# Expert stage of a graph and expert layer: slots of 128 lanes in split float32r, or two experts of 64 seats side by side in native float32

## The chip, the cores and the metric

The kernel runs on one core of one Trainium2 chip (trn2). The metric is the device time of one execution in microseconds. Of the kernel before there are three runs: 924.34, 924.97 and 926.14 us, median 924.97 us.

## The reference

The layer takes x, 384 tokens of 1024 float32, and 12288 typed edges. After a layer norm it adds an attention over the graph (16 heads, a mask built from the edges) and a linear attention with elu features to x. Then a mixture of experts is added to the layer norm of that sum:

```python
sel_logits = jnp.einsum('nd,ed->ne', xt, expert_sel)
gates = jax.nn.sigmoid(sel_logits)
sel_val, sel_idx = jax.lax.top_k(gates, N_HEADS)
gate_full = jnp.zeros_like(gates).at[jnp.arange(N)[:, None], sel_idx].set(sel_val)
scores = jax.nn.relu(jnp.einsum('nd,edf->nef', xt, keys))
scores = scores * gate_full[:, :, None]
out = jnp.einsum('nef,efv->nv', scores, values)
```

There are 32 experts, each with keys of 1024x512 and values of 512x1024 in float32 (2.1 MB each, 4.2 MB together), and each of the 384 tokens goes to 4 of them: 1536 places. On the inputs used, the reference's own routing gives four experts 65, 65, 69 and 84 tokens, and the other 28 at most 56.

## The kernel before

The work runs in one order on all engines: eleven projections of 1024x1024 weights, the attention, the last projections (o0 and o1), a router, and the expert stage. Weights come through SyncE's DMA queue (SP) in chunks of 1 MB. float32 weights and activations are each split in two float32r parts, a high part that ScalarE (ACT) copies and a low part that VectorE (DVE) gets by subtraction; `mm3` (lines 1210 to 1214) multiplies high by high, high by low and low by high, three matmuls for one.

**Router** (lines 1097 to 1161 on DVE). It counts the tokens of each expert and gives each expert one slot of 128 lanes, and a further one for every 128 tokens more. No expert has over 128 tokens, so there are 32 slots. A table says for each slot which token sits in which lane (`gidx`) and with what gate (`tabf`). `slotx` has the expert of each slot, `slots` the loop's end.

**Expert stage, by slots.** For slot s:
- POOL gathers the slot's rows of the normed tokens from HBM by an indirect DMA (`gather`, L643 to L646) into `xg`.
- PE turns them (`x_T`, L1434: eight 128x128 transposes). ACT and DVE evict them as a high and a low part (`xgTh`, `xgTl`).
- `do_keys` (L1419): eight blocks of `mm3` with 512 columns. ACT takes relu and gate (`hsb`), PE turns that (`h_T`, L1440: four transposes), ACT and DVE split it (`hTh`, `hTl`).
- `do_values` (L1424), once for each half of the 1024 outputs: four blocks of `mm3` each.
- ACT evicts y (`ysb`, L828), and POOL adds it to the rows of `out` in HBM by an indirect DMA that adds (L654), masked by lane.

Each megabyte of weights is split by ACT (L724) and DVE (L953), two quarter instructions a chunk, ahead of the matmuls. `pe_slot` (L1443) writes the order out: keys of slot s+1, `x_T` of slot s+2, values of slot s with `h_T` of slot s+1 in their midst. The loop takes two slots a round.

**Chunks.** There are 8 chunk buffers (`raw` and `raw_x`) and 8 split buffers. SP loads the first four expert chunks as soon as the last projection's chunks are split, the next four when the attention is done (`s_pv`), and the others as buffers are split (L536, L564). Between them `rows_out` writes `acc` (the sum before the experts) to `out` and the normed rows to `xt_dram`.

**Attention.** Here native float32 matmuls stand already. `values_of` (L459 to L465) multiplies for two heads at a time, with 128x64 weights each, one head's result in the partitions 0 to 63 of a PSUM bank and the other's in 64 to 127, 384 columns:

```python
for c in range(NT):
    for side in range(2):
        h = 2 * hp + side
        last = nc.tensor.matmul(ps[7][head_rows(side), 0:N], v2[:, c, h * HD:(h + 1) * HD], pT[:, h % PTS, c, :],
                                start=(c == 0), stop=(c == NT - 1))
```

Of the kernel before, what the change touches and what calls it, by code (L numbers as in the profile page):

```python
# [14 lines left out]
P = 128  # L15
# [35 lines left out]
AHEAD = 4  # L51
STEPS = PAIRS * NT
XRAW = 8
XSUB = 8
XLEAD = 4
LANE_STEP = 16
# [48 lines left out]
def gps_layer_kernel(nc, x, edges, etw, W, cols, rows, selT, keys, values, C, xt_dram, out):  # L105
# [3 lines left out]
    with ctx:  # L109
# [9 lines left out]
        arena = sb("arena", [P, 3 * 6144 + 3 * 3072 + 32 + NT * N + D], F32)  # L119
# [7 lines left out]
        BIV = MASK + NT * N * 4  # L127
        xnh, xnl = at("xnh", [P, DC, N], FR, A0), at("xnl", [P, DC, N], FR, A0 + 12 * KB)
# [25 lines left out]
        raw_x = [at(f"raw_x{r}", [P, 4, HALF], F32, A1 + 8 * KB * r) for r in range(3)] + [at("raw_x3", [P, 4, HALF], F32, F2)]  # L154
        wh_x = [at(f"wh_x{r}", [P, 2, HALF], FR, A0 + 8 * KB * r)[:, :, :] for r in range(3)]
        wl_x = [at(f"wl_x{r}", [P, 2, HALF], FR, A0 + 8 * KB * r + 4 * KB)[:, :, :] for r in range(3)]
        xgTh = [at(f"xgTh{p}", [P, DC, P], FR, A2 + 8 * KB * p) for p in range(2)]
        xgTl = [at(f"xgTl{p}", [P, DC, P], FR, A2 + 8 * KB * p + 4 * KB) for p in range(2)]
        hTh = [at(f"hTh{p}", [P, EF, P], FR, A2 + 16 * KB + 4 * KB * p) for p in range(2)]
        hTl = [at(f"hTl{p}", [P, EF, P], FR, A2 + 18 * KB + 4 * KB * p) for p in range(2)]  # L160
# [14 lines left out]
        inslot_h = at("inslot_h", [P, NT, TOPK, SLOTS], F16, route + 7 * KB)  # L175
        slot1h_h = at("slot1h_h", [P, NT, TOPK, SLOTS], F16, route + 9 * KB)
        picked = at("picked", [P, NT, TOPK, NE], F32, route + 11 * KB)
        lane1h_h = at("lane1h_h", [P, NT * TOPK, P], F16, route + 13 * KB)
        cmp = at("cmp", [P, SLOTS - NE, NE], F32, F1)
        lane1h = at("lane1h", [P, NT * TOPK, P], F32, F1 + 2 * KB)  # L180
        tabf = at("tabf", [P, SLOTS], F32, F2 + 8 * KB)
        m8 = at("m8", [P, NT, 8], F32, F2 + 8 * KB + 256)
        pos = at("pos", [P, 4, NT * TOPK], F32, F2 + 8 * KB + 384)
        gidx = at("gidx", [P, SLOTS], I32, F2 + 9 * KB)
        slotx = at("slotx", [P, SLOTS], I32, F2 + 9 * KB + 256)
        slot1h = at("slot1h", [P, NT, TOPK, SLOTS], F32, F2 + 9 * KB + 512)
        acc = sb("acc", [P, NT, D], F32)
        raw = sb("raw", [P, RAW, 4, HALF], F32)
        wh = sb("wh", [P, SUB, 2, HALF], FR)
        wl = sb("wl", [P, SUB, 2, HALF], FR)  # L190
# [4 lines left out]
        wh_x.append(at("wh_x3", [P, 2, HALF], FR, MASK)[:, :, :])  # L195
        wl_x.append(at("wl_x3", [P, 2, HALF], FR, BIV)[:, :, :])
        ysb = [at("ysb0", [P, D], F32, F1 + 8 * KB)[:, :], etmp[:, :, :].rearrange("p a b -> p (a b)")]
# [27 lines left out]
        pcol = sb("pcol", [P, 1], I32)  # L225
# [5 lines left out]
        x_banks = banks[:, 2:4, :].rearrange("p b (c t) -> p (b c) t", t=P)  # L231
        y_banks = [banks[:, 4 + 2 * p:6 + 2 * p, :].rearrange("p b n -> p (b n)") for p in range(2)]
# [4 lines left out]
        s_load = [sem(f"s_load{r}") for r in range(XRAW)]  # L237
# [51 lines left out]
        s_x0h = sem("s_x0h")  # L289
        s_x0l = sem("s_x0l")  # L290
# [5 lines left out]
        s_xhi = sem("s_xhi")  # L296
        s_xlo = sem("s_xlo")
        s_h = sem("s_h")
        s_hT = sem("s_hT")
        s_hhi = sem("s_hhi")  # L300
        s_hlo = sem("s_hlo")
        s_ye = sem("s_ye")
        s_sc = sem("s_sc")
        s_scd = sem("s_scd")
# [7 lines left out]
        def nth_split(s):  # L312

            return s + 1 + (AHEAD if s >= jobs["o1"]["sub"] else 0)

        def nth_expert_split(k):
            return (jobs["o1"]["sub"] if k < AHEAD else SUBS) + k + 1

# [12 lines left out]
        def attention_act(act, split_out, split_ahead):  # L331
# [24 lines left out]
            for i in range(STEPS + 6):  # L356
                if 0 <= i - 3 < STEPS:
                    turned_even(i - 3)
                if i < STEPS:
                    exps(2 * i)  # L360
                    exps(2 * i + 1)
                if 0 <= i - 1 < STEPS and normed_by_act(2 * i - 1):
                    normed(2 * i - 1)
                if i == SPLIT_STEP:
                    split_out()
                if i - 4 == STEPS - 1:
                    act.wait_ge(s_t, 2 * STEPS)
                    split_ahead()
                if 0 <= i - 4 < STEPS and (i - 4) % NT == NT - 1:
                    pair_hi((i - 4) // NT)  # L370
# [21 lines left out]
        def attention_dve(dve, split_out, split_ahead):  # L392
# [13 lines left out]
            for i in range(STEPS + 6):  # L406
# [10 lines left out]
                if i - 5 == STEPS - 1:  # L417
                    split_ahead()
# [89 lines left out]
        raw_of = [raw[:, r, :, :] for r in range(RAW)] + [t[:, :, :] for t in raw_x]  # L508
        wh_of = wh_x + [wh[:, r, :, :] for r in range(SUB)]
        wl_of = wl_x + [wl[:, r, :, :] for r in range(SUB)]  # L510
# [3 lines left out]

        def x_load_done(c, j):

            r = c % XRAW
            return 16 * ((CHUNKS // RAW if r < RAW else 0) + c // XRAW + 1) + 16 * j


        @block.sync
        def _(sp):
# [12 lines left out]
            def expert_half(src_ap, e, half, c):  # L535
                sp.dma_start(raw_of[c % XRAW], src_ap[bass.ds(e, 1), half].rearrange("a p k n -> p (a k) n"))\  # L536
                    .then_inc(s_load[c % XRAW], 16)

            def expert_chunks(src_ap, e, c, j):

                for half in range(2):
                    sp.wait_ge(s_lo, SUBS + 2 * (c + half - XRAW + 1) + 16 * j)
                    expert_half(src_ap, e, half, c + half)


            def rows_out(sp):
                for t in range(NT):
                    sp.wait_ge(s_free, o1_done + t)
                    sp.dma_start(out[t * P:(t + 1) * P, :], acc[:, t, :]).then_inc(s_out, 16)
# [3 lines left out]
            ahead = [src_ap[e, half] for src_ap, e in ((keys, 0), (keys, 1), (values, 0), (keys, 2), (values, 1), (keys, 3))  # L553
                     for half in range(2)]
            for c, chunk in enumerate(ahead):
                if c < RAW:
                    sp.wait_ge(s_lo, nth_split(2 * (CHUNKS + c - RAW) + 1))
                elif c == RAW:
                    sp.wait_ge(s_pv, PAIRS)
                elif c >= XRAW:  # L560
                    if c == XRAW + 2:
                        rows_out(sp)
                    sp.wait_ge(s_lo, nth_expert_split(2 * (c - XRAW) + 1))
                sp.dma_start(raw_of[c % XRAW], chunk).then_inc(s_load[c % XRAW], 16)  # L564
            sp.wait_ge(s_slots, 1)
            last = sp.value_load(slots[0:1, 0:1], min_val=PAIRS_MIN - 1, max_val=PAIRS_MAX - 1)
            c = len(ahead)
            with sp.Fori(0, last - 1) as j:

                e = [sp.value_load(slotx[0:1, bass.ds(2 * j + q, 1)], min_val=0, max_val=NE - 1) for q in range(2, 6)]  # L570
                expert_chunks(values, e[0], c, j)
                expert_chunks(keys, e[2], c + 2, j)
                expert_chunks(values, e[1], c + 4, j)
                expert_chunks(keys, e[3], c + 6, j)
            e = [sp.value_load(slotx[0:1, bass.ds(2 * last + q, 1)], min_val=0, max_val=NE - 1) for q in range(2)]
            expert_chunks(values, e[0], c, last - 1)
            expert_chunks(values, e[1], c + 2, last - 1)
# [3 lines left out]
        def _(pool):  # L581
# [66 lines left out]
            def pool_slot(j, p, count, ahead):  # L648
                s = 2 * j + p
                nc.gpsimd.tensor_copy(pcol[:, :], gidx[:, bass.ds(s, 1)]).then_inc(s_pch, 1)  # L650
                pool_wait(s_pch, count + 1)
                pool_wait(s_ye, s + 3)
# [3 lines left out]
                if ahead:  # L656
                    pool_wait(s_xT, s + 3)
                    gather(s + 4, p, count + 2)
                pool_wait(s_sc, 16 * s + 16)
                pool.sem_inc(s_scd, 1)  # L660

# [10 lines left out]
            last = pool.value_load(slots[0:1, 0:1], min_val=PAIRS_MIN - 1, max_val=PAIRS_MAX - 1)  # L672
            pool.sem_inc(s_scd, 2)
            pool.wait_ge(s_out, 16 * NT)
            pool.wait_ge(s_xT, 1)
            gather(2, 0, 4)
            pool.wait_ge(s_xT, 2)
            gather(3, 1, 5)
            with pool.Fori(0, last) as j:
                for p in range(2):  # L680
                    pool_slot(j, p, 4 * j + 2 * p + 5, True)
# [840 lines left out]
```

## Time and profile before

| | |
|---|---|
| median of 3 runs | 924.97 us |
| span of the profiled execution, first to last instruction | 920.8 us |
| PE busy | 878.7 us (95%) |
| PE weight loads busy | 736.1 us (80%) |
| DVE busy | 655.5 us (71%) |
| ACT busy | 536.9 us (58%) |
| POOL busy | 333.4 us (36%) |
| DMA, mean over the span | 227 GB/s, 209.36 MB |

The profile gives one execution by its span; it has no total time of its own, so the span is set against the median of the runs. The attention ends at about 442 us, o1 at 467 us, and the expert stage's first matmul starts at 497 us. PE is busy nearly everywhere, so its share says little of a single stage; the stage from 497 us on is read by its windows and by the order of PE's instructions. A matmul's duration in the profile is longer than its distance to the next, since matmuls are pipelined: where they stand back to back the distance from start to start is what counts. A native float32 matmul stands in the trace as two records.

### The profile page before, as it was taken

The numbers are of one execution on the slowest core, as the hardware profiler recorded it, in microseconds if no ns is written. First come the engines' busy times: TensorE is split into PE (matmuls) and PEld (weight loads), VectorE is DVE, ScalarE is ACT, GpSimd is POOL, SyncE is SP. The second block draws the span as 40 slices with busy tenths as digits, with TensorE's granted clock in tenths as the row PEclk, the third lists the DMA queues.
The fourth block names the chain that finished last, engine by engine and source line by source line (L and its number), as shares of the span: only waits on it lengthen the run. The fifth ranks groups of instructions, "written<-read, shape, count | busy, mean of one in ns | idle before, by whom it ended". The sixth has DMA issues, their size and how long they took to land.

```text
span 920.8 us, 13930 instructions
## 1 busy us (share of the span) xinstructions
PE 878.7 (95%) x4462; PEld 736.1 (80%) x4462; DVE 655.5 (71%) x1040; ACT 536.9 (58%) x701; POOL 333.4 (36%) x295
## 2 busy tenths in 40 slices
PE   6999999999999999999989989999999999999992
PEld 6987888889889999655766868887888888888882
DVE  7589857534344543685776969889889889989980
ACT  3454312423323322686333968888888888898870
POOL 2042344444444100686003324443324444333341
PEclk9999999999999999999988989999999999999997
DMA  9935432243333533110482989999999999999931
GB/s 353 375 137 183 138 138 92 92 138 138 98 132 138 188 98 132 47 47 1 151 352 76 359 300 343 360 370 362 358 359 359 367 362 370 361 363 365 359 110 22
DMA packets 41638, 209.36 MB, mean 227 GB/s; under 512 B 13136, under 2 KB 13520, under 8 KB 18816
## 3 DMA queue, kind: packets, MB, share of 16 engines
q1 hardware_dynamic: 26496, 186.66, 53.5%
q0 software_dynamic: 14240, 21.38, 8.4%
q10 hardware_dynamic: 864, 0.83, 0.3%
q8 instruction: 22, 0.36, 0.2%
q14 instruction: 16, 0.13, 0.0%
HBM read 209.63 MB, written 21.20 MB: 251 GB/s over the span
## 4 chain that ended last, share of the span: by engine, by line
PE 75%; DMA 11%; DVE 5%; POOL 3%; issue 3%; ACT 1%; POOLq 0%; ACTq 0%; DVEq 0%
PE ps L1212 22%; PE ps L1214 21%; PE ps L1213 21%; DMA out_dram<-etmp,pcol 3%; DMA xg<-xt_dram,gcol 3%; DMA out_dram<-ysb,pcol 3%; PE ps L1434 3%; PE ps L463 2%; POOL out_dram L654 1%; PE ps L439 1%; PE ps L452 1%; PE ps L1440 1%; POOL pr L429 1%; PE ps L1294 1%; DMA ei<-in_edges 1%
## 5 line engine op out<-in xcount | busy, mean ns | idle before, releaser
L714 ACT ACTIVATE wh<-raw 128x1024 fp32r<-128x1024 f32 x88 | 93.0, 1060 | 208.0 <-PE ps L1214 207.7
L896 DVE TENSOR_TENSOR wl<-raw,wh 128x1024 fp32r<-128x1024 f32 x88 | 108.1, 1229 | 131.5 <-ACT wh L714 131.1
L627 POOL DMA_INDIRECT plane<-code,idx x96 | 99.8, 1040 | 122.4 <-DMA plane<-code,idx 96.5
L1212 PE MATMUL ps<-wh_x,hTh 128*128 128x512 f32 x248 | 103.5, 417 | 0.0
L1212 PE MATMUL ps<-wh,xgTh 128*128 128x512 f32 x248 | 98.2, 396 | 0.0
L1214 PE MATMUL ps<-wh_x,hTl 128*128 128x512 f32 x248 | 98.2, 396 | 0.0
L1213 PE MATMUL ps<-wl,xgTh 128*128 128x512 f32 x248 | 97.9, 395 | 0.0
L1214 PE MATMUL ps<-wh,xgTl 128*128 128x512 f32 x248 | 97.8, 394 | 0.0
L1213 PE MATMUL ps<-wl_x,hTh 128*128 128x512 f32 x248 | 97.8, 394 | 0.0
L1212 PE MATMUL ps<-xnh,wh 128*128 128x384 f32 x256 | 86.8, 339 | 0.9 <-DVE xnl L1002 0.9
L1214 PE MATMUL ps<-xnh,wl 128*128 128x384 f32 x256 | 86.6, 338 | 0.0
L1213 PE MATMUL ps<-xnl,wh 128*128 128x384 f32 x256 | 86.4, 338 | 0.0
L953 DVE TENSOR_TENSOR wl<-raw,wh 128x1024 fp32r<-128x1024 f32 x64 | 76.2, 1223 | 12.3 <-ACT wh L724 12.1
L953 DVE TENSOR_TENSOR wl<-raw_x,wh 128x1024 fp32r<-128x1024 f32 x64 | 76.3, 1223 | 11.5 <-ACT wh L724 11.4
L953 DVE TENSOR_TENSOR wl_x<-raw,wh_x 128x1024 fp32r<-128x1024 f32 x64 | 76.7, 1219 | 5.1 <-ACT wh_x L724 4.8
L953 DVE TENSOR_TENSOR wl_x<-raw_x,wh_x 128x1024 fp32r<-128x1024 f32 x64 | 76.4, 1217 | 2.8 <-ACT wh_x L724 2.7
L650 POOL COPY pcol<-gidx 128x1 int32 x32 | 17.7, 552 | 162.4 <-DMA out_dram<-etmp,pcol 81.9
L429 POOL TENSOR_SCALAR pr<-pr,mx 128x384 f32<-128x384 f32 x40 | 49.3, 1252 | 74.1 <-DVE mx L390 74.1
L724 ACT ACTIVATE wh_x<-raw 128x1024 fp32r<-128x1024 f32 x64 | 67.6, 1061 | 14.2 <-PE ps L1214 13.8
L724 ACT ACTIVATE wh_x<-raw_x 128x1024 fp32r<-128x1024 f32 x64 | 67.4, 1060 | 12.1 <-PE ps L1214 10.7
L724 ACT ACTIVATE wh<-raw 128x1024 fp32r<-128x1024 f32 x64 | 65.6, 1055 | 10.7 <-PE ps L1214 10.2
L724 ACT ACTIVATE wh<-raw_x 128x1024 fp32r<-128x1024 f32 x64 | 65.7, 1054 | 9.6 <-PE ps L1214 9.0
(230 smaller groups left out, 2023.9 us busy)
## 6 DMA issues: line engine op xcount, KB each, us to landing
raw<-in_keys SPq DMA_DIRECT2D x34, 1024.0 KB
raw_x<-in_values SPq DMA_DIRECT2D x34, 1024.0 KB
raw_x<-in_keys SPq DMA_DIRECT2D x30, 1024.0 KB
raw<-in_values SPq DMA_DIRECT2D x30, 1024.0 KB
raw<-in_w_v SPq DMA_DIRECT2D x8, 1024.0 KB
raw<-in_w_q SPq DMA_DIRECT2D x8, 1024.0 KB
raw<-in_w_k SPq DMA_DIRECT2D x8, 1024.0 KB
key_rows<-key_dram POOLq DMA_DIRECT2D x6, 1024.0 KB, 5.9
```

The costliest lines, as they stand in the source:

```text
L429: nc.gpsimd.tensor_scalar(pr[:, u % RING, :], pr[:, u % RING, :], mx[:, 3, u:u + 1], None, ALU.mult).then_inc(s_p, 1)
L463: last = nc.tensor.matmul(ps[7][head_rows(side), 0:N], v2[:, c, h * HD:(h + 1) * HD], pT[:, h % PTS, c, :], start=(c == 0), stop=(c == NT ...
L627: nc.gpsimd.indirect_dma_start(plane[m], bass.IndirectOffsetOnAxis(idx[:, g:g + 1].bitcast(U32), 0), code[:, g:g + 1], None, bounds_check= ...
L650: nc.gpsimd.tensor_copy(pcol[:, :], gidx[:, bass.ds(s, 1)]).then_inc(s_pch, 1)
L714: nc.scalar.activation(wh[:, s % SUB], raw[:, c % RAW, 2 * (s % 2):2 * (s % 2) + 2, :], ACT.Copy)\
L724: nc.scalar.activation(wh_of[k % XSUB], raw_of[c % XRAW][:, 2 * (k % 2):2 * (k % 2) + 2, :], ACT.Copy)\
L896: nc.vector.tensor_tensor(wl[:, s % SUB], raw[:, (s // 2) % RAW, 2 * (s % 2):2 * (s % 2) + 2, :], wh[:, s % SUB].bitcast(F32), ALU.subtrac ...
L953: nc.vector.tensor_tensor(wl_of[k % XSUB], raw_of[(k // 2) % XRAW][:, 2 * (k % 2):2 * (k % 2) + 2, :], wh_of[k % XSUB].bitcast(F32), ALU.s ...
L1212: nc.tensor.matmul(o, ah, bh_, start=start, stop=False)
L1213: nc.tensor.matmul(o, ah, bl_, start=False, stop=False)
L1214: return nc.tensor.matmul(o, al, bh_, start=False, stop=stop)
L1434: last = nc.tensor.transpose(ps[2 + b // 4][:, (b % 4) * P:(b % 4 + 1) * P], xg[p][:, b * P:(b + 1) * P], ident[:, :])
```

## The change

- Experts get seats of 64 lanes in place of slots of 128. The seats are rounded up to a multiple of four (a round of the loop). Two seats make a pair: lanes 0 to 63 are one expert's, 64 to 127 the other's. The gather and the transposes go by pairs.
- Keys and values are multiplied in native float32, without a split of weights or activations: for each block one matmul with 128x64 weights for each of the two experts, into the two halves of one PSUM bank (`two_experts`).
- The ring has 16 chunk buffers of 1 MB in place of 8. `raw`, `wh` and `wl` move into the arena and serve as part of it. Loads wait for `s_spent` (the chunk's matmuls), and start for the first eight at the attention's end.
- y is no longer added in HBM. It is split in float32r parts, and `put` multiplies a 0/1 matrix (`place`, lane to token, made by DVE) with both parts: six groups of two matmuls of 512 columns for each pair, standing between the key blocks of the pair after next (those of the last two pairs at the end). DVE adds each into `acc` on chip (`y_add`). `out` is written at the end, in six DMAs of 256 KB. The write of `acc` ahead of the experts goes.

The diff, cut to its core:

```diff
-SLOTS_MAX = (N * TOPK) // P + NE - 1
-PAIRS_MIN, PAIRS_MAX = NE // 2, (SLOTS_MAX + 1) // 2
-SLOTS = 2 * PAIRS_MAX + 2
+LANES = 64
+SEATS_MAX = (N * TOPK) // LANES + NE - 1
+ROUNDS_MIN, ROUNDS_MAX = NE // 4, (SEATS_MAX + 3) // 4
+SEATS = 4 * ROUNDS_MAX
+PAIRS_OF_SEATS = 2 * ROUNDS_MAX
-XRAW = 8
-XSUB = 8
+XRING = 16
...
+            sp.wait_ge(s_pv, PAIRS)
             for c, chunk in enumerate(ahead):
+                if 8 <= c < 12:
+                    sp.wait_ge(s_lo, nth_split(2 * (CHUNKS - RAW + c - 8) + 1))
+                elif c == 12:
+                    rows_out(sp)
+                    sp.wait_ge(s_used, SUBS)
+                elif c >= XRING:
+                    sp.wait_ge(s_spent, spent(c))
+                sp.dma_start(ring[c % XRING], chunk).then_inc(s_ring[c % XRING], 16)
...
+            for v in range(2):
+                for t in range(NT):
+                    sp.wait_ge(s_add, 12 * prev + 18 + 3 * v + t + 1)
+                    cs = slice(v * HALF, (v + 1) * HALF)
+                    sp.dma_start(out[t * P:(t + 1) * P, cs], acc[:, t, cs]).then_inc(s_out, 16)
...
-                nc.gpsimd.indirect_dma_start(out, bass.IndirectOffsetOnAxis(pcol[:, :].bitcast(U32), 0), ysb[p], None,
-                                             bounds_check=N - 1, oob_is_err=False, compute_op=ALU.add).then_inc(s_sc, 16)
...
+            with pool.Fori(0, prev + 1) as j:
                 for p in range(2):
+                    pool_wait(s_xT, 2 * j + p + 1)
+                    gather(2 * j + p + 2, p, 2 * j + p + 4)
...
+            def act_slot(s, p, first=False, x_ahead=True):
+                h_evict(s + 1)
+                if x_ahead:
+                    x_evict(s + 2, p)
+                y_hi(s, 0, first)
+                hT_evict(s + 1, 1 - p)
+                y_hi(s, 1, first)
...
-            for t in range(2, NT):
-                rlink(nc.vector.scalar_tensor_tensor(small[:, 1, :], tot, t * P + 0.5, small[:, 1, :], ALU.is_gt, ALU.add))
+            for t in range(2, N // LANES):
+                rlink(nc.vector.scalar_tensor_tensor(small[:, 1, :], tot, t * LANES + 0.5, small[:, 1, :], ALU.is_gt, ALU.add))
...
+            def dve_slot(s, p, first=False, x_ahead=True):
+                if not first:
+                    for g in range(6):
+                        y_add(s - 1, g)
+                if x_ahead:
+                    x_evict(s + 2, p)
+                place_of(s, p)
+                for v in range(2):
+                    y_lo(s, v)
...
+            def two_experts(c, j, to, what, k, kc, first, fin):
+
+                for side in range(2):
+                    half = slice(LANES * side, LANES * side + LANES)
+                    if kc == 0:
+                        pe.wait_ge(s_ring[(c + side) % XRING], ring_landed(c + side, j))
+                    last = nc.tensor.matmul(to[half, :], what[:, k, half], ring[(c + side) % XRING][:, kc, :], start=first, stop=fin)
+                if kc == 3:
+                    last.then_inc(s_spent, 1)
+
+            def put(s, g, p):
+
+                v, t = g // NT, g % NT
...
+                to = place[p][:, t * P:(t + 1) * P]
+                nc.tensor.matmul(ps[6 + g % 2], to, yh[:, v, :], start=True, stop=False)
+                nc.tensor.matmul(ps[6 + g % 2], to, yl[:, v, :], start=False, stop=True).then_inc(s_put, 1)
+
+            def do_keys(s, c, j, p, put_of=None):
...
+                for k in range(DC):
+                    if k == DC // 2:
+                        pe.wait_ge(s_xd, s + 1)
+                    two_experts(c + 2 * (k // 4), j, ps[0], xgT[p], k, k % 4, k == 0, k == DC - 1)
+                    if put_of is not None and 1 <= k <= 6:
+                        put(put_of, k - 1, p)
...
+            def pe_slot(s, j, p, x_ahead=True):
+
+                do_keys(s + 1, 4 + 8 * p, j, 1 - p, None if isinstance(s, int) and s == 0 else s - 1)
+                if x_ahead:
+                    x_T(s + 2, p, 16 * j + 32)
+                do_values(s, 8 + 8 * p, j, p, 0)
+                h_T(s + 1)
+                do_values(s, 8 + 8 * p, j, p, 1)
```

## Rows read from the trace of the kernel before

**Rows 1.** The page: busy time by engine, and GB/s in 40 slices of 23 us.

```profile
PE 878.7 (95%) x4462; PEld 736.1 (80%) x4462; DVE 655.5 (71%) x1040; ACT 536.9 (58%) x701; POOL 333.4 (36%) x295
GB/s 353 375 137 183 138 138 92 92 138 138 98 132 138 188 98 132 47 47 1 151 352 76 359 300 343 360 370 362 358 359 359 367 362 370 361 363 365 359 110 22
```

**Rows 2.** Windows: length, busy PE, PEld, DVE, ACT, POOL, clock, DMA share, GB/s.

```profile
494.00:498.00 4.00, 4.00 (x15) 2.68 (x15) 1.40 (x3) 1.08 (x2) 1.20 (x2) 0.57 0.77 290
...
600.00:880.00 280.00, 278.76 (x1341) 228.88 (x1340) 250.75 (x224) 246.44 (x268) 110.63 (x91) 1.00 0.99 361
```

**Rows 3.** Waits, 600 to 880 us: who waited for whom, total, times, longest.

```profile
ACT wh_x L724 <- PE ps L1214: 17.6, 67, 0.4
...
ACT wh L724 <- DMA raw<-in_keys: 0.5, 1, 0.5
```

**Rows 4.** Timeline of PE in a slot: start, length, engine, line, operation.

```profile
768.01 0.39 PE L1214 MATMUL ps<-wh,xgTl 128*128 128x512 f32 x1
768.25 1.03 PE L1434 MATMUL ps<-c_all,xg 128*128 128x128 f32 x8
...
780.69 1.03 PE L1434 MATMUL ps<-c_all,xg 128*128 128x128 f32 x8
```

**Rows 5.** Timeline of PE at the stage's end.

```profile
904.08 0.40 PE L1214 MATMUL ps<-wh,hTl 128*128 128x512 f32 x1
```

**Rows 6.** PE's groups by form: weights' shape, output's shape, count, busy us, mean ns.

```profile
L1212 PE MATMUL ps<-wh,xgTh 128*128 128x512 f32 x248 | 98.2, 396 | 0.0
...
L1212 PE MATMUL ps<-xnh,wh 128*128 128x384 f32 x256 | 86.8, 339 | 0.9 <-DVE xnl L1002 0.9
...
L463 PE MATMUL ps<-pT,v 128*64 128x384 f32 x96 | 17.2, 494 | 0.2 <-issue 0.2
```

**Rows 7.** Timeline of PE around one burst of `values_of`, standing among float32r matmuls.

```profile
439.17 0.39 PE L1213 MATMUL ps<-wl,mbh 128*128 128x512 f32 x1
439.40 0.40 PE L1214 MATMUL ps<-wh,mbl 128*128 128x512 f32 x1
439.73 2.16 PE L463 MATMUL ps<-pT,v 128*64 128x384 f32 x12
441.81 0.50 PE L1212 MATMUL ps<-wh,mbh 128*128 128x512 f32 x1
442.15 0.39 PE L1213 MATMUL ps<-wl,mbh 128*128 128x512 f32 x1
```

**Rows 8.** Timeline of PE's weight loads in the same burst.

```profile
440.10 0.14 PEld L463 LDWEIGHTS ps<-pT,v 128*64 128x64 f32 x2 [0.18 <-issue]
440.42 0.14 PEld L463 LDWEIGHTS ps<-pT,v 128*64 128x64 f32 x2 [0.18 <-issue]
```

**Rows 9.** Windows in which nearly only weights are loaded (columns as in rows 2).

```profile
458.00:462.00 4.00, 4.00 (x19) 3.22 (x18) 3.13 (x15) 0.00 (x0) 0.00 (x0) 1.00 1.01 426
...
514.00:518.00 4.00, 4.00 (x21) 3.26 (x21) 4.00 (x5) 3.26 (x5) 0.00 (x0) 1.00 1.01 428
```

**Rows 10.** The page's DMA queues: packets, MB, share of the 16 engines' span.

```profile
q1 hardware_dynamic: 26496, 186.66, 53.5%
q0 software_dynamic: 14240, 21.38, 8.4%
```

**Rows 11.** Timeline of the router and the start of the expert stage.

```profile
480.99 0.19 DVE L1119 SCALAR_TENSOR_TENSOR small<-ps,small 128x32 f32<-128x32 f32 x1
...
489.35 1.51 POOL L669 DMA_INDIRECT xg<-xt_dram,gidx  x1 [4.42 <-DVE gidx L1150]
...
495.75 0.60 ACT L850 ACTIVATE xgTh<-ps 128x512 fp32r<-128x512 f32 x1 [6.94 <-PE ps L1434]
...
496.38 0.69 DVE L1191 TENSOR_TENSOR xgTl<-ps,xgTh 128x512 fp32r<-128x512 f32 x1 [2.94 <-ACT xgTh L850]
...
497.13 0.63 PE L1212 MATMUL ps<-wh_x,xgTh 128*128 128x512 f32 x1
```

**Rows 12.** DMA issues: size and median us to landing.

```profile
acc<-in_x SPq DMA_DIRECT2D x3, 512.0 KB, 5.1
```

More of the change, by code:

```diff
@@ L565, in _ @@
             sp.wait_ge(s_slots, 1)
-            last = sp.value_load(slots[0:1, 0:1], min_val=PAIRS_MIN - 1, max_val=PAIRS_MAX - 1)
+            prev = sp.value_load(slots[0:1, 0:1], min_val=ROUNDS_MIN - 2, max_val=ROUNDS_MAX - 2)
             c = len(ahead)
[L568 to L574, printed above, removed]
@@ L575, in _ @@
-            e = [sp.value_load(slotx[0:1, bass.ds(2 * last + q, 1)], min_val=0, max_val=NE - 1) for q in range(2)]
-            expert_chunks(values, e[0], c, last - 1)
-            expert_chunks(values, e[1], c + 2, last - 1)
+            with sp.Fori(0, prev) as j:
+                e = [sp.value_load(slotx[0:1, bass.ds(4 * j + q, 1)], min_val=0, max_val=NE - 1) for q in range(4, 12)]
+                expert_chunks(values, e[0], e[1], c, j)
+                expert_chunks(keys, e[4], e[5], c + 4, j)
+                expert_chunks(values, e[2], e[3], c + 8, j)
+                expert_chunks(keys, e[6], e[7], c + 12, j)
@@ L739, in _ @@
                 if name == "att":
-                    attention_act(act, lambda: split(jobs["o0"]["sub_end"]), lambda: [split_expert(k, 0) for k in range(AHEAD)])
+                    attention_act(act, lambda: split(jobs["o0"]["sub_end"]))
                     continue
@@ L801, in _ @@
             gate_exp(2)
-            for k in range(4, 4 + XLEAD):
-                split_expert(k, 0)
             act.wait_ge(s_token, 1)
@@ L855, in _, with x_evict, keys_spent, h_evict @@
-            act.wait_ge(s_gate, 2)
-            h_out(SUBS + 4, 0)
-            h_hi(1, 0)
-            for k in range(10, 12):
-                split_expert(k, 0)
-            with act.Fori(0, last) as j:
+            def x_evict(s, p):
+                act.wait_ge(s_xT, s + 1)
+                nc.scalar.activation(xgT[p][:, 0:4, :], x_halves[0], ACT.Copy).then_inc(s_xa, 1)
+            def keys_spent(s):
+                return 2 if isinstance(s, int) and s == 0 else 4 * s
+            def h_evict(s):
+                act.wait_ge(s_spent, keys_spent(s))
+                nc.scalar.activation(hsb[:, :], ps[0][:, :], ACT.Relu, scale=tabf[:, bass.ds(s, 1)]).then_inc(s_h, 1)
@@ L861, in _ @@
+            hT_evict(0, 0)
+            act_slot(0, 0, first=True)
+            act_slot(1, 1)
+            with act.Fori(1, prev + 1) as j:
                 for p in range(2):
-                    act_slot(j, p, True)
-            act_slot(last, 0, False)
-            y_out(last, 1, SUBS + 16 + 16 * last)
+                    act_slot(2 * j + p, p)
+            act_slot(2 * prev + 2, 0, x_ahead=False)
+            for v in range(2):
+                y_hi(2 * prev + 3, v, after_last=2)
         @block.vector
@@ L1196, in _, with x_evict @@
-            x_lo(2, 1)
-            for k in range(6, 10):
-                split_expert(k, 0)
-            h_lo(1, 0)
-            for k in range(10, 12):
-                split_expert(k, 0)
-            with dve.Fori(0, last) as j:
-                for p in range(2):
-                    dve_slot(j, p, True)
-            dve_slot(last, 0, False)
+            def x_evict(s, p):
+                dve.wait_ge(s_xT, s + 1)
+                nc.vector.tensor_copy(xgT[p][:, 4:8, :], x_halves[1]).then_inc(s_xd, 1)
@@ new lines, in dve_slot @@
+            def dve_slot(s, p, first=False, x_ahead=True):
+                if not first:
+                    for g in range(6):
[3 more added lines that the diff above has]
+                place_of(s, p)
+                for v in range(2):
+                    y_lo(s, v)
+            prev = dve.value_load(slots[0:1, 0:1], min_val=ROUNDS_MIN - 2, max_val=ROUNDS_MAX - 2)
+            x_evict(0, 0)
+            dve.wait_ge(s_r, NT + 4)
@@ new lines, in _ @@
+            nc.vector.tensor_copy(tabf[:, :], ps[6][:, 0:PAIRS_OF_SEATS]).then_inc(s_gate, 1)
+            x_evict(1, 1)
+            dve_slot(0, 0, first=True)
+            dve_slot(1, 1)
+            with dve.Fori(1, prev + 1) as j:
+                for p in range(2):
+                    dve_slot(2 * j + p, p)
+            dve_slot(2 * prev + 2, 0, x_ahead=False)
+            place_of(2 * prev + 3, 1)
+            for g in range(6):
+                y_add(2 * prev + 2, g)
+            for v in range(2):
+                y_lo(2 * prev + 3, v)
@@ L1208, in _ @@
+            for g in range(6):
+                y_add(2 * prev + 3, g)
         @block.tensor
@@ L1432, in x_T, with do_values @@
+            def do_values(s, c, j, p, v):
+                if v == 0:
+                    pe.wait_ge(s_he, s + 1)
+                if not isinstance(s, int) or s >= 1:
+                    pe.wait_ge(s_yl, 2 * s + v - 1)
+                for k in range(EF):
+                    two_experts(c + 2 * v, j, ps[4 + v], hT[p], k, k, k == 0, k == EF - 1)
+            def x_T(s, p, landed):
                 pe.wait_ge(s_g[p], landed)
+                if not isinstance(s, int) or s >= 1:
+                    pe.wait_ge(s_xa, s)
+                    pe.wait_ge(s_xd, s)
```

364 lines of the change are left out of this document (134 added, 230 removed).

## The prediction

> **What bounds the kernel now.** I read first the page: PE is busy 95% of the span, and from slice 24 on the DMA engines move about 360 GB/s [rows 1]. So either could set the pace of the expert stage. The windows say the same of 600 to 880 us: PE 278.76 of 280 us, clock 1.00, DMA share 0.99 [rows 2]. The waits decide: ACT, which stands between the loads and PE, waits 17.6 us for PE in one of its groups and once, for 0.5 us, for a chunk [rows 3]. PE is the bound, DMA close behind. The order of PE's instructions then gives the price of a slot: `x_T` starts at 768.25 and, one slot later, at 780.69, so 12.44 us a slot [rows 4]. A float32r matmul of 512 columns starts 0.232 us after the one before it (439.17 to 439.40, 768.01 to 768.25) [rows 4, 7]; 48 of them are 11.1 us, and the twelve transposes with what they break are the other 1.34 us. The stage's matmuls run from 497.13 [rows 11] to 904.48 [rows 5], 407.3 us; 32 slots are 398, and 9 us are stalls early on. After the last matmul come 16.3 us in which POOL adds the last rows in HBM, to the span's end at 920.8.
>
> **How much work there is after.** By the routing, four experts need two seats and 28 need one: 36 seats, 9 rounds of four, 18 pairs. Before, 32 slots. The weights to load grow from 134 to 151 MB.
>
> **PE, part by part.**
> - Keys and values. A pair has 8 key blocks and 2 x 4 value blocks, so 16 steps of two native float32 matmuls of 128x64 weights and 512 columns. The same form stands in the attention, with 384 columns. Its 12 records (6 matmuls) take 2.08 us from 439.73 to 441.81 [rows 7], and their weights come two records at a time every 0.32 to 0.33 us [rows 8]. A native record lasts 494 ns where a float32r record of 384 columns lasts 339, and one of 512 columns 396 [rows 6]: 128 columns are 57 ns, so the 155 ns more are about one more pass over 384 columns. A record alone would then hold the array for 0.32 us, and two go through in that time: the two halves overlap. With 512 columns that is 0.325 x 512/384 = 0.433 us for two records and 0.867 us a step. The other end is 2.08/12 scaled to 512 columns, 0.924 us a step, which counts the burst's edges in. I take 0.867, and the edges by themselves. 18 x 16 = 288 steps are 249.7 us (at 0.924: 266).
> - Edges. Between a float32r matmul and the burst pass 0.33 in place of 0.23 us, the burst takes 2.08 in place of 6 x 0.325 = 1.95, and the float32r matmul behind it 0.34 in place of 0.23 (441.81 to 442.15): 0.10 + 0.13 + 0.10, about 0.33 us a burst [rows 7]. If what is lost is one record without a partner, it grows with the columns to 0.43. Bounds: nothing, if the trace's edges belong to the waits there, and 0.43. Key steps are parted by six `put`s, and values by `x_T` and `h_T`, so a slot has 8 bursts, and with the first and last ones there are about 134. At 0.36, between the two readings, 48 us (0 to 58).
> - `put`: 18 x 12 float32r matmuls x 0.232 = 50.0 us [rows 7].
> - Transposes: 18 x 1.34 = 24.1 us. The splits of weights on ACT and DVE (2 of each a chunk) go altogether; they lay beside PE and freed nothing on it.
> - Sum 372 us. It replaces 407.3 us. By pair it is 20.7 us, where two slots were 24.9.
>
> At the edges a rule speaks against this change. The trace has the next float32r weight load start only at the burst's end, and 0.33 us lost in each burst. The Trainium skill, TensorEngine Tiling (Array Packing), Key Properties, says that changing the tiling mode drains TensorE, which six `put`s a pair do twelve times more. By that rule the edges stay at full price (48 us here); without it the stage would be 324 us and PE no longer the bound. The row decides for the price.
>
> **What lies around it.** The router gets three more DVE steps of 0.19 us on its chain, and smaller tables; +0.4 us, so the first matmul starts at 497.5, in place of 497.13 [rows 11]. The chunks 12 to 15 queue behind 1.6 MB of `xt_dram` from about 474 us and are in by 488, before the gather at 489.35; should they collide with it, 2 us. Just before, from 494 to 498 us, the granted clock was 0.57 [rows 2], so the first steps may run slow: +1. `y_add` (six of 0.69 us, by the like DVE subtraction), the y split (0.60 on ACT, 0.69 on DVE, twice) and `x_evict` are some 7 us of DVE and 4 us of ACT a pair of 20.7 [rows 11]: hidden, unless a `put` waits for its bank. Two banks alternate and a step plus a `put` is 1.3 us, over the 0.69 of an add. POOL loses the adding DMA and its wait, so a gather is issued as soon as its buffer is turned, 20 us before its use.
>
> Tail: `y_hi` 0.60, `y_lo` 0.69, three `put`s 1.4 and the last add 0.69, semaphores between, then 256 KB to HBM, at most the 5.1 us of 512 KB [rows 12]: 9 us.
>
> **Sum.** 497.5 + 1 + 372 + 9 = 879.5 us of span, against 920.8. The runs' median stands 4.2 us above the span (924.97 against 920.8); with that, **884 us**.
>
> **DMA beside it.** Weights alone move at 426 to 428 GB/s [rows 9], so a pair's 8.39 MB are 19.7 us. Its gather is 0.35 MB: 0.8 us at that rate, 1.3 us at the rate of the software queue (21.38 MB in 8.4% of the span) [rows 10]. That makes 20.7 us, just PE's pace. But 16 chunks, two pairs' worth, are on chip before the first matmul, so DMA has 16 pairs to load while PE does 18. It gets free buffers from 502 us: 502 + 16 x 20.7 = 833 us, and with the last steps and the tail 846. The bad end is the 361 GB/s of the old loop [rows 2]: 24.2 us a pair, 502 + 387 + 13 = 902. The old rate had the adding DMAs in it, and four chunks (9.8 us) plus at most the software queue's 77 us over 32 slots (2.4 us) fill its 12.44 us, so I take the fast end, under PE's.
>
> **The rivals.**
> 1. Edges cost little, and DMA sets the pace: PE would be done by 832, DMA at 846, with some stutter 850 to 870, so 855 to 873 us. For it: 0.33 us was read where PE also changed from one precision to another. Chance 0.20.
> 2. Steps at 0.924 with edges at 0.43, or DMA at 361 GB/s: 497.5 + 1 + 266 + 58 + 50 + 24 + 9 = 906 or 902, so 892 to 915 us. Chance 0.20. It is a part of "faster".
> 3. Slower than before: the two halves do not overlap in this stream, since the two matmuls of a side go one behind the other and a `put` follows each step. A record is then 2 x 0.232 = 0.463 us, 64 of them 29.6 us a pair, 533 in place of 250 us, and the time about 1150 us. It decides from 1.01 us a step: 920.8 - 9 - 498.5 - 50 - 24 - 48 = 291 us for 288 steps. Against it: the attention's weights came in twos every 0.325 us. For it: there six matmuls stood together, here mostly one pair between two `put`s. Chance 0.08. The Trainium skill, FP8 and Floating Point Precision, TensorE Precision Notes, has true float32 as four passes through the array; that is the cost of this rival and agrees with the 494 ns record.
> 4. Seats other than 36, a tenth round say, would add two pairs, 41 us: 925 us, no change. The counts 65 and 65 could fall by one without changing the 9 rounds, and none of the rest is near 64. 0.02.
>
> **How the numbers follow.** Forecast 0.50 (875 to 892 us), rival 1 0.20, rival 2 0.20, rival 3 0.08, rival 4 0.02. A measurement of this kernel can tell about 0.2%, 1.8 us. Faster 0.90, within 0.2% 0.02, slower 0.08. The range takes in the forecast, most of rival 1 and most of rival 2: 860 to 912 us.
>
> **What would show it.** In the profile after: PE busy through the stage at clock 1.00, `two_experts` steps 0.87 us apart inside the values, 0.33 to 0.43 us lost around each `put`, about 20.7 us from one `x_T` to the next, no `ACT ... L724` or `L953` after 497 us, DMA near 420 GB/s. Were PE waiting for ring chunks, rival 1 or the bad end holds, told apart by the GB/s. Steps of 1.7 us are rival 3. I am wrong if `x_T` to `x_T` is far from 20.7 with the parts as priced, which would be a wait that I have not seen (a `put` for its bank or for `y_lo`).

## The result and the profile after

The changed kernel takes 871.5 us in the median of four runs (870.4 to 873.1), the kernel before 924.65 us beside it: ratio 0.9425, 95% interval 0.9408 to 0.9442. Forecast were 884 us and a range of 860 to 912. The profiled execution took 872.25 us, its span is 870.4 us.

The page after, as in [rows 1, 10]:

```profile
PE 846.5 (97%) x4126; PEld 534.6 (61%) x4126; DVE 413.4 (47%) x903; ACT 237.4 (27%) x406; POOL 193.2 (22%) x199
GB/s 348 402 166 145 161 131 97 97 107 136 137 107 146 130 167 121 121 0 1 2 231 413 235 364 424 425 427 424 427 425 427 426 427 425 427 424 427 424 107 73
q1 hardware_dynamic: 29232, 203.44, 57.8%
q0 software_dynamic: 7328, 15.05, 4.8%
```

Windows of the expert stage after (length, busy PE, PEld, DVE, ACT, POOL, clock, DMA share, GB/s), to set beside [rows 2]:

```profile
600.00:800.00 200.00, 200.00 (x856) 67.25 (x854) 63.39 (x97) 28.50 (x48) 11.11 (x19) 1.00 1.01 426
800.00:830.00 30.00, 30.00 (x136) 10.54 (x134) 9.30 (x15) 5.36 (x9) 0.00 (x0) 1.00 1.01 427
830.00:870.00 40.00, 35.56 (x144) 12.39 (x140) 15.80 (x25) 4.16 (x7) 0.00 (x0) 1.00 0.16 63
```

PE is busy throughout at full clock, and DMA moves 426 GB/s until about 832 us. Both look like the bound; which one it is the windows can't say, but the last row hints at it: DMA is done 38 us before the end. The timeline of PE shows what a pair consists of:

```profile
704.18 0.66 PE L1423 MATMUL ps<-c_all,hsb 128*128 128x128 f32 x4
704.77 3.65 PE L1372 MATMUL ps<-ring,hT 128*64 128x512 f32 x16
708.25 1.89 PE L1372 MATMUL ps<-ring,xgT 128*64 128x512 f32 x8
710.07 0.50 PE L1386 MATMUL ps<-yh,place 128*128 128x512 f32 x1
710.40 0.40 PE L1387 MATMUL ps<-yl,place 128*128 128x512 f32 x1
710.73 1.08 PE L1372 MATMUL ps<-ring,xgT 128*64 128x512 f32 x4
711.74 0.50 PE L1386 MATMUL ps<-yh,place 128*128 128x512 f32 x1
```

L1372 is `two_experts`, four records a step. Four value steps take 3.48 us (704.77 to 708.25), 0.87 us each. A lone step between two `put`s takes 1.01 us (710.73 to 711.74), a `put` 0.66, and from `put` to `put` it is 1.67 us: 0.87 + 0.46 of work and 0.34 of edges. The chain gives the pair:

```profile
699.64 1.02 PE ps L1415 x8
720.17 1.02 PE ps L1415 x8
740.71 1.02 PE ps L1415 x8
```

`x_T` to `x_T` is 20.53 us. The waits of PE's weight loads from 498 us on (total, times, longest) hold no ring chunk; two of the rows:

```profile
PEld ps L1372 <- issue: 131.0, 443, 0.8
PEld ps L1386 <- DVE acc L1131: 67.8, 86, 1.3
```

The second looks like a cost of the on-chip sum. It is not: at 711.74 the load stands behind a step that is still in the array, and `put`s follow each other 1.67 us apart whether this wait is named or not.

**Where the 50.4 us of span went.** The stage's first and last steps, and the `put` behind them:

```profile
498.96 7.09 PE L1372 MATMUL ps<-ring,xgT 128*64 128x512 f32 x32
858.64 3.65 PE L1372 MATMUL ps<-ring,hT 128*64 128x512 f32 x16
862.22 0.50 PE L1386 MATMUL ps<-yh,place 128*128 128x512 f32 x1
```

The first expert matmul starts at 498.96 us in place of 497.13 [rows 11], +1.8. From it to the end of the last value matmul (862.3 us) are 363.3 us in place of 407.3, -44.0. What follows is 8.1 us in place of 16.3, -8.2. It has the last pair's six `put`s in it.

### The profile page after: what moved, and what is told of

Read it like the earlier page. It is cut to its first block, busy times and chain, and to the rows that moved or that the text cites. A ratio compares the mean times of both kernels' runs of the same rounds, so it can differ in the third digit from the quotient of the medians.

```text
span 870.4 us, 11821 instructions
## 1 busy us (share of the span) xinstructions
PE 846.5 (97%) x4126; PEld 534.6 (61%) x4126; DVE 413.4 (47%) x903; ACT 237.4 (27%) x406; POOL 193.2 (22%) x199
## 4 chain that ended last, share of the span: by engine, by line
PE 89%; DVE 6%; issue 1%; DMA 1%; ACT 1%; POOL 1%; DVEq 0%; ACTq 0%; POOLq 0%
PE ps L1372 31%; PE ps L1167 13%; PE ps L1169 13%; PE ps L1168 13%; PE ps L1386 5%; PE ps L1387 3%; PE ps L1415 2%; PE ps L458 2%; PE ps L434 1%; PE ps L447 1%; PE ps L1423 1%; POOL pr L424 1%; PE ps L1249 1%; DMA ei<-in_edges 1%; DVE wl L852 1%
## 5 line engine op out<-in xcount | busy, mean ns | idle before, releaser
L852 DVE TENSOR_TENSOR wl<-raw,wh 128x1024 fp32r<-128x1024 f32 x88 | 108.1, 1230 | 131.9 <-ACT wh L688 131.5
L688 ACT ACTIVATE wh<-raw 128x1024 fp32r<-128x1024 f32 x88 | 93.0, 1060 | 210.4 <-PE ps L1169 210.1
L1372 PE MATMUL ps<-ring,xgT 128*64 128x512 f32 x576 | 147.9, 609 | 0.2 <-ACT xgT L778 0.2
L1131 DVE TENSOR_TENSOR acc<-ps,acc 128x512 f32<-128x512 f32 x108 | 74.1, 691 | 98.7 <-PE ps L1387 98.7
L1386 PEld LDWEIGHTS ps<-yh,place 128*128 128x128 f32 x108 | 20.1, 186 | 84.1 <-DVE acc L1131 67.8
L1372 PEld LDWEIGHTS ps<-ring,xgT 128*64 128x64 f32 x576 | 32.6, 135 | 62.7 <-issue 62.3
L1372 PE MATMUL ps<-ring,hT 128*64 128x512 f32 x288 | 65.7, 598 | 0.0
L1372 PE MATMUL ps<-raw,hT 128*64 128x512 f32 x288 | 65.7, 598 | 0.0
L1386 PE MATMUL ps<-yh,place 128*128 128x512 f32 x108 | 53.8, 498 | 1.6 <-DVE acc L1131 1.6
L1167 PEld LDWEIGHTS ps<-xnh,wh 128*128 128x128 f32 x256 | 48.1, 188 | 1.4 <-DVE xnl L952 1.2
L1168 PEld LDWEIGHTS ps<-xnl,wh 128*128 128x128 f32 x256 | 48.1, 188 | 0.1
L1169 PEld LDWEIGHTS ps<-xnh,wl 128*128 128x128 f32 x256 | 48.1, 188 | 0.0
```

The lines of the kernel that those rows point to most:

```text
L688: nc.scalar.activation(wh[:, s % SUB], raw[:, c % RAW, 2 * (s % 2):2 * (s % 2) + 2, :], ACT.Copy)\
L852: nc.vector.tensor_tensor(wl[:, s % SUB], raw[:, (s // 2) % RAW, 2 * (s % 2):2 * (s % 2) + 2, :], wh[:, s % SUB].bitcast(F32), ALU.subtrac ...
L1131: nc.vector.tensor_tensor(rows_of, ps[6 + g % 2], rows_of, ALU.add).then_inc(s_add, 1)
L1167: nc.tensor.matmul(o, ah, bh_, start=start, stop=False)
L1168: nc.tensor.matmul(o, ah, bl_, start=False, stop=False)
L1169: return nc.tensor.matmul(o, al, bh_, start=False, stop=stop)
```

## The experiments

Times are medians; the kernel before stood at 924.5 to 928.1 us beside them.

### Do the two halves work at once?

```diff
-                for k in range(EF):
-                    two_experts(c + 2 * v, j, ps[4 + v], hT[p], k, k, k == 0, k == EF - 1)
+                for side in range(2):
+                    for k in range(EF):
+                        one_expert(c + 2 * v, j, ps[4 + v], hT[p], k, k, side, k == 0, k == EF - 1)
```

The keys go alike: four blocks of one side, then four of the other.

> The changed kernel with the same matmuls in another order: four of one expert, then four of the other, in place of one of each in turn. If the step of 0.87 us comes from two halves of the array working at once (my theory), a record now has a partner only where the sides meet, a step goes to about 1.6 to 1.73 us, x_T to x_T from 20.4 to about 33 us and the time to about 1080 to 1120 us. If the records simply take 0.217 us one behind the other (rival), the order is without effect: 870 us.

Measured: 1019.8 us, one run. The same matmuls in another order cost 148 us. Timeline of PE:

```profile
709.42 0.40 PE L1386 MATMUL ps<-yl,place 128*128 128x512 f32 x1
709.74 1.93 PE L1371 MATMUL ps<-ring,xgT 128*64 128x512 f32 x4
711.60 0.50 PE L1385 MATMUL ps<-yh,place 128*128 128x512 f32 x1
```

Four records of one side take 1.86 us, where four of alternating sides take 1.01: 4 x 0.43 and 2 x 0.43 us, each with 0.13 to 0.14 of edge. So the halves overlap, a record holds its half for 0.43 us, and the edge does not come from a record without a partner. The time stayed under the 1080 us expected, because sides also meet at the seams:

```profile
695.00 1.09 PE L1417 MATMUL ps<-c_all,xg 128*128 128x128 f32 x8
724.22 1.09 PE L1417 MATMUL ps<-c_all,xg 128*128 128x128 f32 x8
```

A pair takes 29.2 us. With no overlap at all it would be 20.5 + 32 x 0.433 = 34.4 us. A pair has three seams without a `put` or a transpose between the sides; four records side by side at each are 12 x 0.433 = 5.2 us, which is the difference. At a seam the next side's records run beside the last ones of the side before:

```profile
705.50 0.64 PE L1371 MATMUL ps<-ring,xgT 128*64 128x512 f32 x1
705.93 0.59 PE L1371 MATMUL ps<-raw,hT 128*64 128x512 f32 x1
705.98 0.59 PE L1371 MATMUL ps<-ring,xgT 128*64 128x512 f32 x1
706.36 0.59 PE L1371 MATMUL ps<-raw,hT 128*64 128x512 f32 x1
706.41 0.59 PE L1371 MATMUL ps<-ring,xgT 128*64 128x512 f32 x1
706.78 0.59 PE L1371 MATMUL ps<-raw,hT 128*64 128x512 f32 x1
```

### What is an edge?

Two kernels with the same work in a `put`, 0.87 us of array, which differ in the weights' shape alone:

```diff
-                nc.tensor.matmul(ps[6 + g % 2], to, yh[:, v, :], start=True, stop=False)
-                nc.tensor.matmul(ps[6 + g % 2], to, yl[:, v, :], start=False, stop=True).then_inc(s_put, 1)
+                for side in range(2):
+                    half = slice(LANES * side, LANES * side + LANES)
+                    last = nc.tensor.matmul(ps[6 + g % 2][half, :], to[:, half].bitcast(F32), yh[:, v, :].bitcast(F32), start=True, stop=True)
+                last.then_inc(s_put, 1)
```

```diff
+                nc.tensor.matmul(ps[6 + g % 2], to.bitcast(F32), yh[:, v, :].bitcast(F32), start=True, stop=True).then_inc(s_put, 1)
```

The second edit stands in place of the same two lines. In both kernels the high part of y and `place` are written as float32, and the low part is not multiplied.

> The changed kernel with y and the 0/1 matrix kept as float32 and each put as two native float32 matmuls of 128x64 weights side by side (the low part of y has nothing left in it and is not multiplied). A put is then 4 records, 0.87 us, like a key step, in place of 0.46 us. If the 0.34 us at the edges is the change between 128x64 and 128x128 weights, it goes: from put to put 0.87 + 0.87 = 1.73 us (was 1.67), x_T to x_T about 20.7 us, time 877. If the edges come from something else (waits, other banks), 2.07 us from put to put, x_T to x_T 22.8 us and time 912 to 915.

> As the kernel with native puts in halves, but each put is one native float32 matmul of 128x128 weights: two records of 0.43 us, and again 0.87 us of array. If the edge is the change of the weights' shape, 0.87 + 0.87 + 0.34 = 2.07 us from put to put, x_T to x_T 22.8 us, time 912 to 915. If the edge is the change from float32 to float32r, it is absent here: 1.73 us, 877.

Measured, one run each: 879.3 us in halves, 911.2 us whole. Timeline in halves (L1388 the `put`):

```profile
713.34 1.03 PE L1388 MATMUL ps<-yh,place 128*64 128x512 f32 x4
714.20 1.03 PE L1372 MATMUL ps<-ring,xgT 128*64 128x512 f32 x4
715.06 1.03 PE L1388 MATMUL ps<-yh,place 128*64 128x512 f32 x4
```

and whole (L1386):

```profile
709.02 1.13 PE L1386 MATMUL ps<-yh,place 128*128 128x512 f32 x2
710.08 1.08 PE L1372 MATMUL ps<-ring,xgT 128*64 128x512 f32 x4
711.08 1.13 PE L1386 MATMUL ps<-yh,place 128*128 128x512 f32 x2
```

In halves 1.72 us from `put` to `put`, no edge at all, with the same semaphore waits in the program; whole 2.06 us, 0.33 of edge, though nothing changes its precision. The edge is the change between 128x64 and 128x128 weights. The Trainium skill's rule that a change of the tiling mode drains TensorE (TensorEngine Tiling (Array Packing), Key Properties) fits these two kernels.

### Is PE's order of instructions the bound, or DMA?

Puts by twos behind key blocks 1, 3 and 5:

```diff
-                    if put_of is not None and 1 <= k <= 6:
-                        put(put_of, k - 1, p)
+                    if put_of is not None and k in (1, 3, 5):
+                        put(put_of, k - 1, p)
+                        put(put_of, k, p)
```

> The six puts of a pair go two at a time behind key blocks 1, 3 and 5, so three bursts fewer a pair. If PE's order of instructions sets the time and an edge costs 0.34 us, x_T to x_T falls from 20.37 by 1.02 to 19.35 us, PE would end 16 us sooner, at about 848 of span, and DMA, whose last chunk lands near 832, ends at 845 at the earliest: 848 to 852 us of time. If DMA sets the pace already (share 1.01 at 426 GB/s from 540 us on), the time stays at 870. If a put behind a put waits for its bank, the pair falls by less than 1 us.

Puts beside the transposes, which have 128x128 weights too:

```diff
+                    if put_of is not None and k == 3:
+                        put(put_of, 0, p)
+                        put(put_of, 1, p)
...
                 if x_ahead:
                     x_T(s + 2, p, 16 * j + 32)
+                if put_of is not None:
+                    put(put_of, 2, 1 - p)
+                    put(put_of, 3, 1 - p)
                 do_values(s, 8 + 8 * p, j, p, 0)
                 h_T(s + 1)
+                if put_of is not None:
+                    put(put_of, 4, 1 - p)
+                    put(put_of, 5, 1 - p)
```

> Two puts behind key block 3, two behind x_T, two behind h_T: five bursts fewer a pair than in the changed kernel. PE alone would need 20.37 - 5 x 0.34 = 18.7 us a pair and end near 838; DMA's end near 832 plus the last steps and the tail makes 845 to 848 of span, 846 to 850 us of time. PE then waits for chunks for the first time (some 10 us in total). If DMA set the pace before: 870.

Key matmuls with 256 columns, half of the keys' product left out:

```diff
+                    w = slice(0, 256 if what is xgT[0] or what is xgT[1] else 512)
-                    last = nc.tensor.matmul(to[half, :], what[:, k, half], ring[(c + side) % XRING][:, kc, :], start=first, stop=fin)
+                    last = nc.tensor.matmul(to[half, w], what[:, k, half], ring[(c + side) % XRING][:, kc, w], start=first, stop=fin)
```

> The changed kernel with the key matmuls over the first 256 of 512 columns (half of the keys' product is left out); all loads, waits and puts stay. PE alone needs 20.37 - 8 x 0.43 = 16.9 us a pair. If PE set the time until here, the time falls to DMA's own pace: 832 for the last chunk, 3 us of steps, 8 us of tail, span 843 to 846 us, with x_T to x_T at 8 chunks of 2.46 us plus the gather, 20.4 to 20.8 us. If DMA set the pace already, 870 as it is. If a shorter keys part frees chunks sooner and DMA has room, below 840.

Measured: by twos 855.15 us (853.4 to 857.0, four runs), expected 848 to 852; beside the transposes 850.95 us (849.4 to 852.3, four runs; ratio to before 0.9197, interval 0.9162 to 0.9231); 256 columns 851.2 us, one run. Pieces of the chain, by twos (`x_T` is L1416):

```profile
711.33 1.02 PE ps L1416 x8
730.80 1.02 PE ps L1416 x8
```

and beside the transposes:

```profile
588.23 1.02 PE ps L1416 x8
607.03 1.02 PE ps L1416 x8
```

20.53 us became 19.47 (three edges fewer, 0.35 each) and 18.80 (five fewer, 0.35 each). The kernel by twos came 3 us over its expectation: that had started from 20.37 us a pair, and in the profiled run the first eight steps began 0.8 us later and took 7.93 us in place of 7.02. With five edges fewer PE begins to wait for chunks, and with 256 columns it waits far more. Waits for chunks, the first row of the kernel beside the transposes:

```profile
PEld ps L1372 <- DMA ring<-in_keys: 3.1, 5, 0.9
```

and of the kernel with 256 columns:

```profile
PEld ps L1373 <- DMA ring<-in_keys: 30.0, 23, 2.9
```

Yet both have the same time, and in both the last chunks land near 832 us, as in the changed kernel. There PE was the bound, and 20 us below it lies DMA's floor at about 850 us.

### What the chunks on chip are worth

No chunk before the router is done:

```diff
+            rows_out(sp)
+            sp.wait_ge(s_used, SUBS)
+            sp.wait_ge(s_slots, 1)
             for c, chunk in enumerate(ahead):
...
```

> The changed kernel, but no expert chunk is loaded before the router has set the loop's end (about 492.7 us); so nothing is on chip when the expert stage starts. DMA's work of 144 chunks at 2.58 us (with the gathers) then starts at 493 and ends at 864; with the last steps and the tail 875 of span, 5 us slower than the changed kernel, PE waiting for chunks throughout. If DMA sets the pace in the changed kernel already, the loss is the whole prefetch of 16 chunks, some 40 us: 910.

Measured: 883.6 us, one run, span 881.8. Timeline of PE at its start:

```profile
497.56 1.07 PE L1372 MATMUL ps<-ring,xgT 128*64 128x512 f32 x2
500.48 5.35 PE L1372 MATMUL ps<-ring,xgT 128*64 128x512 f32 x16 [1.85 <-DMA ring<-in_keys]
506.39 3.65 PE L1372 MATMUL ps<-ring,xgT 128*64 128x512 f32 x14 [0.56 <-DMA ring<-in_keys]
```

11.4 us more, against 5 expected by my theory and 40 by the other. DMA moved 426 GB/s until about 862 us, as expected. The mistake was to let it set the end: PE lost its time at the start, with 9.9 us of waits for chunks before 545 us and 0.5 us after, and then went its 20.53 us a pair (later pairs at 813.70 and 834.24), so the loss stayed, and the stage ended at 873.7 us.

Only half of the ring, with the changed kernel's order and with the puts beside the transposes:

```diff
-            return (c - XRING) // 2 + 1
+            return (c - 8) // 2 + 1
...
```

The chunks ahead of the loop wait by the same count.

> The changed kernel with only 8 of the 16 chunks of the ring in use (a load waits until all but 8 are spent). Then one pair's chunks are on chip before the first matmul, DMA restarts at about 502 us with 136 chunks at 2.58 us to go and ends at 853 if it never pauses; with the steps and the tail 864, under PE's 870. If depth matters only by this sum, the time stays within 3 us of 872. If a shallow ring makes PE and DMA wait for each other (a load can only be asked for when four steps are done, and lands 2.5 to 5 us later beside the others), DMA pauses, PE waits, and the time is 880 to 900.

> The kernel with the puts beside the transposes, with only 8 of the 16 chunks of the ring in use. With the changed kernel's order of puts the half ring cost nothing, since PE's 20.53 us a pair left DMA time. Here PE needs 18.8 us, less than DMA's 20.6, so the chunks on chip before the first matmul should count: DMA has 136 chunks to go from 502 us at 2.58 us and ends at 853 in place of 832, and the time is 866 to 872 where the full ring took 851, with PE waiting for chunks some 20 us. If the depth of the ring never mattered, 851.

Measured: 872.55 us (872.2 to 873.0, four runs), within the scatter of the changed kernel, though DMA now moved weights until about 851 us, 19 us longer; and 872.1 us (870.7 to 874.2, four runs) where the full ring took 850.95. Windows of the latter, as above, and its first wait for a chunk:

```profile
700.00:800.00 100.00, 97.78 (x434) 43.22 (x434) 30.39 (x50) 14.89 (x25) 6.01 (x10) 1.00 1.01 426
```

```profile
PEld ps L1370 <- DMA ring<-in_keys: 19.5, 16, 1.9
```

The second half of the ring gives nothing as the change stands, and 21 us once the edges are gone: eight more chunks on chip are 8 x 2.46 = 20 us of DMA (an estimate from 1.05 MB at 426 GB/s).

### The adding DMA, and the last puts

The kernel before without its adding DMA (the output is then the sum before the experts):

```diff
-                nc.gpsimd.indirect_dma_start(out, bass.IndirectOffsetOnAxis(pcol[:, :].bitcast(U32), 0), ysb[p], None,
-                                             bounds_check=N - 1, oob_is_err=False, compute_op=ALU.add).then_inc(s_sc, 16)
+                pool.sem_inc(s_sc, 16)
```

> The kernel before without the indirect DMA that adds y to the rows of out in HBM: the output is the sum before the experts, and only POOL's waits and DMA traffic go. If of the change's 53 us some 9 are the early stalls behind the first adding DMA and some 10 the tail after the last matmul, and the rest PE's matmuls, this kernel takes 903 to 908 us with slots still 12.44 us apart. If the adding DMAs also slowed PE's stream through the loads, slots come closer together and the time is below 895. If neither, 915 and over.

Measured: 906.1 us (905.9 to 906.3, four runs), 18.4 us under the kernel before. Slots stay 12.44 us apart, as in [rows 4]:

```profile
763.35 0.87 PE ps L1433 x8
775.79 0.87 PE ps L1433 x8
```

Its last matmul ends 5 us before the span does, in place of 16.3, and from its first expert matmul (500.39) to its last are 399.0 us in place of 407.3. DMA moved 341 GB/s between 600 and 880 us, at share 0.91, in place of 361 at 0.99, and PE did not notice. So of the change's 53 us some 18 are the adding DMA (early stalls and tail). The other 35 are PE's shorter stream: 363.3 us in place of 399.0, less a tail 3.1 us longer and with a start 1.4 us earlier than in this run.

Last, the six puts of the last pair but one ahead of the last values, in the kernel with the puts beside the transposes:

```diff
+            for g in range(6):
+                put(2 * prev + 2, g, 0)
             do_values(2 * prev + 3, 12, prev + 1, 1, 0)
-            for g in range(6):
-                put(2 * prev + 2, g, 0)
```

> The kernel with the puts beside the transposes, and with the last pair's order changed: the six puts of the pair before stand ahead of its values and not in their midst. PE waits there for the last chunks anyway (the first value half takes 4.8 us in place of 3.6), so 2 to 3 us go: 848 to 849 us where that kernel took 851. If the low part of y is not ready and the puts wait in front of the values, nothing is gained: 850 to 852.

Measured: 852.2 us (849.4 to 853.9, four runs): nothing gained. The six puts take 5.2 us ahead of the values. PE waits 1.22 us in them for a bank: DVE must empty it, and in its order the low part of y (830.34 us) stands first. The values then start at 834.79 us, and the last chunks had landed at about 832.

## Why the prediction was right, and where it was off

- **The bound.** PE before and PE after, with DMA just beneath: right. Making PE's stream shorter alone took 16 to 21 us more off; making loads later cost little more than what PE waited at its start.
- **The halves overlap:** right, at 0.867 us a step, read from 384-column records and scaled. The other order of the same matmuls cost 148 us. Rival 3 is out.
- **The edges:** forecast 0.36, measured 0.34. Of the two readings (a fixed cost, or an unpaired record that grows with the columns) the fixed one holds; I took their middle. That the edge is the change of the weights' shape, the prediction had from a rule beside its row; the two kernels with native puts show it.
- **What was off in the sum** is the PE term: 372 us, where 363.3 passed. The 372 us have all 18 x 6 `put`s in them, but the last six stand in the tail, so 6 x 0.464 = 2.8 us do not belong there. The transposes were priced at 1.34 us a pair, which holds the old loop's own breaks, with the new edges added on top. Without its eight edges a pair's transposes take 20.53 - 13.87 - 2.78 - 2.72 = 1.16 us, 3 us less in all, and the first `x_T` lies ahead of the stage, 0.8 us. Some 131 edges at 0.34 are 3.5 us less than the 48. Against these stand about 1.5 us of waits, most of them for banks between the last `put`s (854.34 to 858.64 us). As an estimate from these rows this makes 8.6 us. With the tail 0.9 us shorter and the start 0.5 us later it is 9.0 of the 9.1 us by which the span was short of 879.5.
- **Around the span** I took 4.2 us from the old kernel (its median less the span of one profiled run). That was the scatter between runs: each run of the kernel before that stands beside the experiments has 1.8 to 1.9 us between its time and its span, and the changed kernel's profiled run has 1.85 and stood 0.7 us above the median. A span of 920.8 us then belongs to a run of some 922.6 us. This is 3 us more of the 12.5 between forecast and median.
- **The start:** 498.96 where 497.5 and 1 us for the low clock were forecast, so 0.5 us late in all, but not for those reasons. The first eight steps took 7.02 us, 0.1 over 8 x 0.867, so the low clock cost next to nothing in this run. The router did not get longer either: from its first transposes to the gather are 22.0 us (468.71 to 490.70), and 22.3 before (467.10 to 489.35). It began 1.6 us later. Between 120 and 130 us the granted clock was 0.83 on average in this run and 1.00 in the one of the kernel before. Over all profiled runs here the router begins at 467.0 to 467.2 us without such a stretch, at 467.9 to 468.7 with one, and at 469.6 to 470.0 with two (10 to 20 us and 120 to 130 us). So two profiles can differ by up to 3 us before the stage begins, whatever the edit.
- **Tail:** 8.1 for 9, but by luck. Three `put`s in 1.4 us were forecast. Six stand there, and from 862.22 us on they take 4.9 us, with 0.9 and 0.2 us of waits for a bank that DVE still had to empty. The write of 256 KB was put at up to 5.1 us and lands after 2.0 in the median. The two errors cancel.
- **The adding DMA:** 9 us of stalls and a longer tail, confirmed by taking it away: 8.3 us off the stage and 11 off the tail.
- **DMA beside it.** A pair in 20.7 us: 8.74 MB at 426 GB/s are 20.5, right. Its end near 833: 832, right. The floor, put at 846 of span, lies at 848 to 849. The bad end of 361 GB/s did not come; the rate was that of plain loads. That the adding DMAs were all that stood in its way is not shown: the old loop without them moves 341 GB/s at share 0.91, which would be some 375 at a full share (an estimate).
- Rival 1 was the wrong mechanism for this kernel (edges did not come cheap), though its time of 855 to 873 holds the result. It came true in the kernel with the puts beside the transposes. Rival 2 did not occur, and rival 4 did not: 18 pairs.

## What to carry to other kernels

In this kernel two native float32 matmuls with 128x64 weights, in the two column halves of the array, go in the time of one, provided that the halves alternate in the order of issue. Every change between 128x64 and 128x128 weights costs 0.34 us there and back: put what has full-width weights together, beside transposes for instance. When two resources both look full, shorten one stream and see: DMA at share 1.01 for 290 us was not the bound, since it ran ahead by what was on chip at the start. A deeper ring is worth its megabytes only where DMA is the slower of the two; the same edit was worth nothing with one order of puts and 21 us with another.

## What was not expected

- At the seams of the order with one side at a time, about four records of the next side ran beside the last four of the side before (705.50 to 706.84 us). So by these rows the array starts records of a free half some four records ahead of their turn. The Trainium skill, TensorE: Matmul & The Clock Gate, Part 3, The mechanism, has matmuls start and end strictly in the order of the program; the record that starts at 705.50 stands behind, in program order, the one that starts at 705.93. Starts in these rows do not keep that order.
- Weights alone, with one gather of 0.35 MB a pair, moved at 426 GB/s for 290 us on end, with the same share of 1.01 as in the short bursts of [rows 9].
